# One transformer layer on one core: the cross-attention sums are turned by a transposing DMA and projected in fp16 pairs, and are normalised straight out of PSUM

## The reference, cut to what matters

```python
q = (x @ Wq).reshape(B, Nq, HEADS, DIM_HEAD).transpose(0, 2, 1, 3)
k = (context @ Wk)...                      # 16 heads of 64
v = (context @ Wv)...
sim = jnp.einsum('bhid,bhjd->bhij', q, k) * SCALE
attn = jax.nn.softmax(sim, axis=-1)
out = jnp.einsum('bhij,bhjd->bhid', attn, v)
out = out.transpose(0, 2, 1, 3).reshape(B, Nq, HEADS * DIM_HEAD)
return out @ Wo + bo
...
x = x + _L0_xattn_ref(_layernorm(x, axis=-1), ctx_768, ...)
```

## Time and profile before

| what | value |
|---|---|
| time, three runs | 2165.36, 2166.11, 2169.33 us, median 2166.11 |
| span of the profiled execution, which is its own time | 2169.9 us |
| mean granted TensorE clock | 0.997 |
| PE busy | 2103.3 us (97%) |
| POOL busy | 1933.6 us (89%) |
| ACT busy | 1832.2 us (84%) |
| DVE busy | 1736.7 us (80%) |
| transfers | 22.10 MB, mean 10 GB/s |

### The profile page before, as it was taken

One profiled execution on the slowest core, in us unless ns is written; L12 is line 12 of the kernel. 1 busy time (PEld: TensorE's weight loads), 2 busy tenths in 40 slices (PEclk: granted clock), 3 DMA queues, 4 the chain that ended last, 5 costly groups with the idle time before them and its releaser, 6 DMA issues.

```text
span 2169.9 us, 58374 instructions
## 1 busy us (share of the span) xinstructions
PE 2103.3 (97%) x22087; PEld 1544.3 (71%) x22087; DVE 1736.7 (80%) x4158; ACT 1832.2 (84%) x3124; POOL 1933.6 (89%) x1127
## 2 busy tenths in 40 slices
PE   8999999999999999999999999999999999999998
PEld 4677777777777777777777777777777777777665
DVE  7778878787887888879687797878878788886764
ACT  6898898989888888998888888898878888888872
POOL 3899999999999899999899998998989999899991
PEclk9999999999999999999999999999999999999999
DMA  3110000000000000000000000000000000000000
GB/s 73 42 38 13 2 13 2 2 13 2 13 2 2 13 2 13 2 13 2 11 13 2 13 2 2 14 2 13 2 11 13 2 13 2 2 2 2 2 11 11
DMA packets 17366, 22.10 MB, mean 10 GB/s; under 512 B 5872, under 2 KB 14976, under 8 KB 17088
## 3 DMA queue, kind: packets, MB, share of 16 engines
q1 hardware_dynamic: 15984, 18.17, 3.0%
q10 hardware_dynamic: 1104, 0.20, 0.1%
HBM read 16.14 MB, written 2.10 MB: 8 GB/s over the span
## 4 chain that ended last, share of the span: by engine, by line
PE 76%; DVE 11%; issue 5%; ACT 5%; POOL 2%; DMA 0%; SPq 0%; DVEq 0%; ACTq 0%; POOLq 0%
PE PS L573 14%; PE PS L613 13%; PE PS L574 13%; PE PS L590 11%; PE PS L592 10%; PE PS L636 4%; DVE EH L1091 4%; PE PS L646 2%; PE PS L623 2%; DVE over L1114 2%; POOL EL L1566 2%; ACT PF L897 2%; PE PS L657 1%; ACT over L919 1%; DVE junk L1359 1%
## 5 line engine op out<-in xcount | busy, mean ns | idle before, releaser
L1566 POOL TENSOR_TENSOR EL<-PF,EH 124x1024 f16<-124x1024 f32 x828 | 1761.7, 2153 | 144.0 <-DVE EH L1091 69.4
L897 ACT ACTIVATE PF<-PS 124x512 f32<-124x512 f32 x1664 | 972.6, 602 | 203.7 <-PE PS L574 190.1
L590 PE MATMUL PS<-Ch,EH 123*128 123x97 f16 (+1 forms) x6656 | 765.8, 207 | 22.9 <-POOL EL L1566 22.2
L592 PE MATMUL PS<-Cl,EL 123*128 123x97 f16 (+1 forms) x6656 | 762.3, 207 | 0.0
L1091 DVE TENSOR_SCALAR_CACHE_REDUCE EH<-PF 124x1024 f16<-124x1024 f32 x621 | 746.1, 1209 | 18.1 <-ACT PF L897 16.9
L590 PEld LDWEIGHTS PS<-Ch,EH 123*128 123x128 f16 (+1 forms) x6656 | 609.1, 98 | 181.5 <-issue 62.7
L1114 DVE CUSTOM_DVE_ANT_1 over<-over,PS 128x806 f32<-128x806 f32 x512 | 506.6, 989 | 284.7 <-ACT over L919 142.8
L592 PEld LDWEIGHTS PS<-Cl,EL 123*128 123x128 f16 (+1 forms) x6656 | 597.8, 98 | 168.2 <-issue 1.9
L573 PE MATMUL PS<-AH,ChT 97*124 97x512 f16 x1664 | 646.6, 389 | 6.5 <-ACT PF L897 5.8
L574 PE MATMUL PS<-AL,ClT 96*124 96x512 f16 x1664 | 633.7, 381 | 0.0
L919 ACT ACTIVATE over<-PS 128x806 f32<-128x806 f32 x512 | 433.4, 846 | 28.6 <-PE PS L613 8.6
(11 more groups left out here) (248 smaller groups left out, 1766.9 us busy)
## 6 DMA issues: line engine op xcount, KB each, us to landing
Cf<-in_ctx SPq DMA_DIRECT2D x16, 546.0 KB
X<-in_x SPq DMA_DIRECT2D x16, 128.0 KB, 2.4
out_x<-X SPq DMA_DIRECT2D x16, 128.0 KB, 1.7
msk<-in_attention_mask SPq DMA_DIRECT2D x4, 256.0 KB, 4.3
AH<-mh SPq DMA_DIRECT2D x63, 2.0 KB
Cf<-in_ctx SPq DMA_DIRECT2D x16, 53.6 KB
xWqT<-in_xWqT SPq DMA_DIRECT2D x2, 256.0 KB, 6.5
xWo<-in_xWo SPq DMA_DIRECT2D x2, 256.0 KB, 4.3
```

The source lines that it names most:

```text
L590: pe.matmul(PS[:, 6, u0:u0 + DC + 1], EH[0:kr, r, qs], Ch[j][0:kr, t, :], start=(t == 0 and q == 0), stop=False, skip_group_check=True)
L592: m = pe.matmul(PS[:, 6, u0:u0 + DC + 1], EL[0:kr, r, qs], Cl[j][0:kr, t, :], start=False, stop=(t == KT - 1), skip_group_check=True)
L897: act.activation(PF[:, n % PRING, :], PS[0:KP, 4 + n % 2, :], ACT.Exp).then_inc(sg("ex"), 1)
L1566: pool.tensor_tensor(EL[:, r - 1:r + 1, :], PF[:, f - 1:f + 1, :], EH[:, r - 1:r + 1, :], ALU.subtract).then_inc(sg("lo_pool"), 1)
```

## The change

- **Normalisation.** The copy `U` goes. VectorE reads the denominators and the sums from PSUM bank 6 itself, directly behind the last value product of a pair (place `n0`), and writes `Un` (fp32, one buffer for each of two pairs). TensorE waits on `un` instead of `u` before the next pair's first value product. The first three value products of a pair are now issued together at its third place, so two steps stand without one.
- **Split.** A new step `u_split` (place `n0+1`, GpSimd `n0+2`): ScalarE writes the high fp16 part of `Un`, GpSimd the low part, into `UHL`.
- **Turn.** `turn_u` is no step of TensorE, ScalarE or PSUM any more. It is one DMA on SP for each quad (place `n0+3`) with `transpose=True`: `UHL`, 128 partitions x 1536 fp16, into `UT`, 12 blocks of 128x128. SP gets an order of its own, with the stores of the output (`c_scat`) six places later.
- **Projection** (place `n0+11`): 12 fp16 products for each quad (high part with `MH`, low part with `ML`, for two row tiles and three blocks) instead of six fp32 ones; VectorE adds to `X` with a scale (`pback`).
- **Once, in the first batch** (places 34 to 39): the maximum of `M`, its power of two, the scaling of `M`, and the split into `MH` and `ML` (VectorE and ScalarE).
- **`sel_rank`.** The sum of two counts and the comparison that makes `keep` are written as `tensor_scalar` with an accumulator output.
- **Closing part.** The last quad goes the same way (`norm` on VectorE as before, then split, DMA, projection); the filler before the last `proj` is 24 products instead of 4 and 1.

The core of the diff:

```diff
+SPLIT_LATER, TURN_LATER, PROJ_LATER = 1, 3, 11
...
-            "ln_stats2": 3, "norm": 3},
+            "ln_stats2": 3, "u_split": 1},
+    "sp": {"c_scat": 6},
...
-        if late >= 1 and late % KT == 1:
+        if late >= 2 and late % KT == 2:
+            put(n, "av", late - 2)
             put(n, "av", late - 1)
-        if late >= 0 and late % KT:
+        if late >= 0 and late % KT >= 2:
             put(n, "av", late)
+        if late >= 0 and late % KT == KT - 1 and late // KT < B * HP - 1:
+            put(n, "norm", late // KT)
...
-        if done >= 2 and (done - 2) % KT == 0:
-            put(n, "norm", (done - 2) // KT)
-        for late, step in ((-2, ("turn_u", 0)), (2, ("turn_u", 1)), (5, ("proj",))):
...
+        if done >= 0 and done % KT == SPLIT_LATER:
+            put(n, "u_split", done // KT)
+        for later, kind in ((TURN_LATER, "turn_u"), (PROJ_LATER, "proj")):
+            if done >= 0 and done % (2 * KT) == KT + later:
+                quad = done // (2 * KT)
+                put(n, kind, quad // QD, quad % QD)
...
-                ("turn_u", B - 1, QD - 1, 0): 4, ("proj", B - 1, QD - 1): 1, ("sel_row", B - 1): 17,
+                ("proj", B - 1, QD - 1): 24, ("sel_row", B - 1): 17,
...
                     if t == 0 and n > 0:
-                        w.wait_ge(sg("u"), b * HP + hp)
+                        w.wait_ge(sg("un"), b * HP + hp)
...
+                    w.wait_ge(sg("ut"), 16 * i)
+                    kb = bank_free(s)
+                    w.wait_ge(sg("m_lo"), 1)
+                    for t in range(T):
                         for c in range(QC):
+                            for part, of in enumerate((MH, ML)):
+                                m = pe.matmul(PS[:, kb, t * D:(t + 1) * D], UT[:, (part * T + t) * QC + c, :],
+                                              of[:, qd * QC + c, :], start=(c == 0 and part == 0),
+                                              stop=(c == QC - 1 and part == 1))
...
+                elif k == "u_split":
+                    w.wait_ge(sg("un"), x + 1)
+                    w.wait_ge(sg("ut"), 16 * max(0, b * QD + qd - 1))
+                    act.activation(UHL[qd % 2][:, 0, :, 2 * (x % 2):2 * (x % 2) + 2, :], Un[x % 2][:, :, :, :],
+                                   ACT.Copy, scale=KEEP).then_inc(sg("uh"), 1)
...
+                elif k == "norm":
                     x, = s.a
                     sums = PS[:, 6, 0:4 * (DC + 1)].rearrange("p (q c) -> p q c", c=DC + 1)
+                    w.wait_ge(sg("av"), (x + 1) * KT)
+                    dve.reciprocal(rden_u[:, x % 2, :], sums[:, :, DC]).then_inc(sg("u_r"), 1)
+                    w.wait_ge(sg("u_r"), x + 1)
+                    if x >= 2:
+                        w.wait_ge(sg("ul"), x - 1)
                     dve.tensor_tensor(
+                        Un[x % 2][:, :, :, :].rearrange("p t h c -> p h t c"),
...
+                        ALU.mult).then_inc(sg("un"), 1)
...
-                    dve.tensor_tensor_reduce(out=rank[:, j, :], in0=cnt[:, j, 0, :], in1=cnt[:, j, 2, :], scale=1.0,
-                                             scalar=0.0, op0=ALU.add, op1=ALU.add, accum_out=spill())
-                    dve.tensor_scalar(keep[:, j, :], cnt[:, j, 1, :], NSEL + 0.5, None,
-                                      ALU.is_gt).then_inc(*own_step())
+                    for t in range(T):
+                        dve.tensor_scalar(rank[:, j, t:t + 1], cnt[:, j, 0, t:t + 1], cnt[:, j, 2, t:t + 1], None,
+                                          ALU.add, ALU.add, accum_out=spill())
+                    dve.tensor_scalar(keep[:, j, :], cnt[:, j, 1, :], NSEL + 0.5, None, ALU.is_gt, ALU.add,
+                                      accum_out=spill()).then_inc(*own_step())
...
+                    w.wait_ge(sg("uh"), x + 1)
+                    pool.tensor_tensor(UHL[qd % 2][:, 1, :, hs, :], Un[x % 2][:, :, :, :], UHL[qd % 2][:, 0, :, hs, :],
+                                       ALU.subtract).then_inc(sg("ul"), 1)
...
+                elif k == "turn_u":
+                    b, qd = s.a
+                    w.wait_ge(sg("ul"), b * HP + 2 * qd + 2)
+                    w.wait_ge(sg("pj_mm"), b * QD + qd)
+                    sp.dma_start(UT[:, :, :], UHL[qd % 2][:, :, :, :, :].rearrange("p w t h c -> p (w t h c)"),
+                                 transpose=True).then_inc(sg("ut"), 16)
```

More of the change, by code:

```diff
@@ L216, in put @@
         stream.append((n + shift.get(kind, 0), len(stream), (kind, *a)))
-    out += opening(engine)
+    out += opening("pe" if engine == "sp" else engine)
     groups, todo = beside_plan(), []
@@ L239, in whole_order @@
         done = n - AV_LAG - (KT - 1)
-        if done >= 2 and (done - 2) % KT == 0:
-            put(n, "norm", (done - 2) // KT)
-        for late, step in ((-2, ("turn_u", 0)), (2, ("turn_u", 1)), (5, ("proj",))):
-            late += KT
-            if done >= late and (done - late) % (2 * KT) == KT:
-                quad = (done - late) // (2 * KT)
-                put(n, step[0], quad // QD, quad % QD, *step[1:])
+        if done >= 0 and done % KT == SPLIT_LATER:
[4 more added lines that the diff above has]
+                put(n, kind, quad // QD, quad % QD)
     out += [step for _, _, step in sorted(stream)]
-    out += [("norm", B * HP - 1), ("turn_u", B - 1, QD - 1, 0), ("turn_u", B - 1, QD - 1, 1), ("proj", B - 1, QD - 1)]
+    out += [("norm", B * HP - 1), ("u_split", B * HP - 1), ("turn_u", B - 1, QD - 1), ("proj", B - 1, QD - 1)]
     out += [("ln_stats2", B - 1), ("sel_w", B - 1), ("sel_row", B - 1)]
@@ L261 @@
     "sa_t": "sa_xT", "sa_qk": "sa_k", "sa_v": "sa_vp", "sa_s": "sa_ex", "sa_turn": "sa_exT", "sa_o": "sa_x1",
-    "sa_f": "x2_lo", "wvo": "crow", "ctx_t": "ct", "q": "q_lo", "placemax": "pm_hi", "turn_u": "ut", "proj": "pj_x",
-    "sigma": "sg_max", "gtop": "gt_max",
+    "sa_f": "x2_lo", "wvo": "crow", "ctx_t": "ct", "q": "q_lo", "placemax": "pm_hi", "proj": "pj_x",
+    "sigma": "sg_max", "gtop": "gt_max", "mtop": "mt_max",
     "sel_row": "sel_cnt", "c_gather": "cg_mr", "c_turn": "c_mrT", "c_qkm": "c_rope", "c_val": "c_vx", "c_tqk": "c_kx",
@@ L395, in build @@
         qscale = sb("qscale", [P, 2, 4, 2])
-        U = [sb(f"U{i}", [P, 4, DC + 1]) for i in range(2)]
-        Un = [sb(f"Un{i}", [P, T, 4, DC]) for i in range(2)]
-        UT = sb("UT", [P, T, QC, P])
+        Un = [sb(f"Un{i}", [P, T, 2, DC]) for i in range(2)]
+        UHL = [sb(f"UHL{i}", [P, 2, T, 4, DC], F16) for i in range(2)]
+        UT = sb("UT", [P, 2 * T * QC, P], F16)
         pmax = sb("pmax", [P, 2, H * T])
@@ L552, in tensor_program @@
                 k, i = s.kind, s.i
-                if (k, *s.a) == ("turn_u", B - 1, QD - 1, 0):
+                if (k, *s.a) == ("proj", B - 1, QD - 1):
                     w.wait_ge(sg("ex"), TOTAL)
@@ L669, in tensor_program @@
                                  ident[0:KP, 0:KP]).then_inc(sg("sg_mm"), 1)
+                elif k == "mtop":
+                    w.wait_ge(sg("mmx"), 1)
+                    kb = bank_free(s)
+                    pe.transpose(PS[:, kb, 0:P], mmx[:, :].to_broadcast([P, P]), ident[:, :]).then_inc(sg("mt_mm"), 1)
                 elif k == "gtop":
@@ L1125, in vector_program @@
                                              op0=ALU.mult, op1=ALU.subtract).then_inc(sg("q_lo"), 1)
-                elif k == "norm" and s.a[0] == LAST_SUMS:
+                elif k == "norm":
                     x, = s.a
                     sums = PS[:, 6, 0:4 * (DC + 1)].rearrange("p (q c) -> p q c", c=DC + 1)
-                    w.wait_ge(sg("av"), TOTAL)
-                    w.wait_ge(sg("un"), x - 1)
-                    dve.reciprocal(rden_u[:, x % 2, :], sums[:, :, DC]).then_inc(*own_step())
-                    w.wait_ge(*own_steps())
-                    w.wait_ge(sg("ut_mm"), T * (B * QD - 2))
+                    w.wait_ge(sg("av"), (x + 1) * KT)
[3 more added lines that the diff above has]
+                        w.wait_ge(sg("ul"), x - 1)
@@ L1151, in vector_program @@
                 elif k == "proj":
                     b, qd = s.a
+                    back = pback[:, b % 2:b % 2 + 1]
+                    if qd == 0:
+                        w.wait_ge(sg("m_back"), 1)
+                        w.wait_ge(sg("sigma"), b + 1)
+                        if b >= 2:
+                            w.wait_ge(sg("pj_x"), at["proj", b - 2, QD - 1])
+                        dve.tensor_scalar(back, u_scale[:, b % 4:b % 4 + 1], mback[:, 0:1], None, ALU.mult, ALU.add,
+                                          accum_out=spill()).then_inc(sg("pj_back"), 1)
@@ L1647, in sync_program @@
             sp.dma_start(rbc[:, :], row("router_b")).then_inc(sg("in_rows"), 16)
-            for s in order:
+            for s in orders["sp"]:
                 k, i = s.kind, s.i
```

114 lines of the change are left out of this document (47 added, 67 removed).

## The result

The changed kernel takes 2243.89 us in the median (2241.81 to 2248.20), the kernel before beside it 2167.72. The ratio is 1.0353 with an interval of 1.0338 to 1.0368: some 77 us slower, where 48 us faster were forecast, and far outside the range of 2066 to 2172. The profiled execution spans 2242.8 us.

The account below looks back on a forecast made before the run. TensorE's issue order was taken as the bound, GpSimd 5% behind. TensorE's relief 66 plus 6 for `keep`, minus 24 of costs, gave 48 us: 2122 profiled, 2118 median, range 2066 to 2172.

Parts of the forecast that it names:

- the 2, 5 and 4 charged against it: Costs in the sum: 2 us for the opening batch, 5 for the closing part, 4 for stepping into the next bound.
- the sums' wait: TensorE's value products wait for the normalisation, or two bare score steps outrun ScalarE: 0.1 us a pair, 13 us.
- `keep`: VectorE's mask instruction loses its wait in accumulator form: 28 us of VectorE; a third of GpSimd's 17 us counted, 6.
- Relief of TensorE: TensorE's issue falls by 90 us, 5.6 a batch; 66 us come through: 8 short batches, 55 long, 3 first and last.
- GpSimd's 5%: GpSimd 95% busy in the short batch, so its work of 120.4 of 126.5 us leaves 6.1 us to gain.
- the length follows PE: From short to long batch TensorE's work grows 4.3 us, GpSimd's 2.4, length 5.7; TensorE's issue order is the bound.
- so no change: On GpSimd the normalising product (0.884 us) goes and the low-part subtraction, taken as 0.88, comes; ends -9 and +30 us.
- ACT's slack: ScalarE's 159.1 us of waiting for TensorE covers its share of the waits behind the split and normalisation.
- the sums' wait eats the gain: Rival: normalisation starts late on VectorE, TensorE stands at each pair's first value product; 2194 us; chance 0.19 with other stream waits.
- The DMA: Turning transfer of 384 KB for each quad lands in 5 us, costing nothing within 7.6 us of cover.
- The rival of the late DMA: Rival: the 12 blocks are turned one after another; landing at 14.4 us gives 2553 us; chance 0.07.
- Opening and closing part: One-time costs: 2 us for scaling and splitting in the opening batch, +4.7 us in the closing chain.

Follow-up runs that it names:

- n4: Changed kernel with GpSimd's low-part subtraction replaced by a one-element copy, the low part a constant zero: 2199.95 us, ratio 1.0134.
- n2: Changed kernel with GpSimd's low part two places later, nothing else: 2220.67 us, ratio 1.0231.
- n17: n4 with its one-element GpSimd copy two places later: ratio 1.0023 to the kernel before.
- n5: Changed kernel with the sums' old road, ranks and mask, low part a constant zero, DMA turn and fp16 projection kept but later: 2167.19 us, ratio 0.9989.
- n11: n5 with the new ranks and mask and a pair's first two value products together at the third step (two bare score steps): ratio 1.0035.
- n9: Kernel before with GpSimd's normalising product cut to a one-element copy, the normalised sums a constant: ratio 0.9963.
- n10: n5 with the new ranks and mask and GpSimd's normalising product cut to a one-element copy: ratio 0.9828.
- n6: Kernel before with only the value products of a pair's first two steps moved together to the third (two bare score steps): 2203.10 us, ratio 1.0158.
- n7: Kernel before with only the new ranks and keep mask (scalar operand and accumulator output): ratio 0.9988.
- n8: Changed kernel with the ranks and keep mask back in their old form: ratio 1.0366 to the kernel before.
- n12: n5 with the new ranks and mask and the normalising product on VectorE as four instructions of 96 columns: 2393.22 us, ratio 1.1033.
- n16: n5 with the new ranks and mask and every second pair's normalising product on ScalarE as four activations of 96 columns: ratio 1.0039.

## Why the prediction was wrong

Four kernels form a square: the low part's work there or not, its place early or late.

| | low part on GpSimd | one element |
|---|---|---|
| as changed | 1.0353 | 1.0134 (n4) |
| two places later on GpSimd | 1.0231 (n2) | 1.0023 (n17) |

The work costs 2.2 and 2.1%, its early place 1.2 and 1.1%, each whatever the other is. With them the loss adds up, in us: turn and fp16 projection -2 (n5); second bare step and the new ranks +10 (n11 to n5); straight normalisation and split against the old copy and GpSimd's product -3 (n17 to n11; the intervals overlap, and turn and projection also stand earlier in n17); the low part at a place where GpSimd stands for ScalarE's high part +24; the low part's work +48. Together +77.

The forecast was -48, so 125 us are missing. The first step below accounts for 53 of them: 66 less the 2, 5 and 4 charged against it make 55, and n5 measured 2. The second and third account for 69: I had nothing, and the runs have -3, +24 and +48. The rest, 3 us, is the sums' wait and `keep`.

- **Relief of TensorE, 66 us of 90 let through: this step failed.** The relief is there: twelve products take 0.67 us (466.22 to 466.89) for 0.69 forecast, and the transposes are gone. But n5 shows that it is worth 2 us beside the full GpSimd, and n9 and n10 that it is worth 29 beside a lighter one. Two readings of the earlier trace rows were wrong. GpSimd's 5% were no room of 6.1 us: its idle time is 6.1 us in the short batch and 9.4 in the long one before, and 5.8 and 9.2 in n5. That is mostly GpSimd standing for VectorE, which a lighter TensorE leaves as it is. And "the length follows PE" was a coincidence of sizes: from the short batch to the long one GpSimd's work grows by 2.4 us and its idle time by 3.3, which is the 5.7 us of length as well, and n5's long batch keeps its length with 4.3 us less of TensorE. For the eleven long batches I took 55 us; n5 has 14 there, and loses most of that again elsewhere. The 4 us for the step into the next bound were the term that should have held nearly all of it.
- **GpSimd, "so no change": this step failed too.** The subtraction took 0.92 us for the 0.88 taken, so in busy time the exchange was even. In time it was not: taking the product off gave 35 us beside n5 (n10), which the straight normalisation with ScalarE's split used up but for 3 (n17 to n11), and the subtraction's 118 us cost 48 (n4).
- **The waits behind `u_split`, for which "ACT's slack" was to cover: failed.** The queue that matters is not ScalarE's but GpSimd's, and its standing for ScalarE's high part is in no term of the sum. It stood 54.5 us in fourteen batches, and TensorE's value products waited 49.0 us for the late remainders, for 17.9. With the low part two places later 24 to 26 us came back (n17, n2).
- **The sums' wait, 13 us: the size right by luck, the mechanism half right.** The second bare step, which the prediction names, costs 10 us beside a lighter TensorE (n11) and 34 beside a full one (n6). The rival "the sums' wait eats the gain" did not come true as told: TensorE waited only 4.6 us for `Un` over the span. It had the sign, not the mechanism.
- **`keep`: the instruction as forecast, the gain not.** It takes 0.149 us now, but `X<-X,keep` behind it went from 348 to 1086 ns in the mean, and in n7 to 1179, so the 28 us of VectorE and the third of 17 us of GpSimd came to next to nothing (n7, n8). VectorE ended 79 us busier, not 45.
- **The DMA: right.** Landed after 3.7 us in the median (5.4 at most) for the 5 taken, far under the cover of 7.6; `proj` waited for one once, 1.40 us, in the closing part. The rival of the late DMA is out. The Trainium skill's figure of 1309 ns for a block (VectorE: DVE Perf Modes, section "The three transpose paths") added up block by block would have given 15.7 us; the runs show that blocks of one transfer don't add up so.
- **Opening and closing part: right.** The first batch took 137.6 us in n5 for 135.0, which is 2.6 where I had 2. In the closing part, from the end of the normalisation (2198.12) to the addition (2204.28) are 6.16 us for the 2.93 of before, +3.2 where I had +4.7.

What stays open: n17 has as light a GpSimd as n10 (1849.2 and 1856.1 us busy) and takes 42 us more. The second bare step is a part of it, somewhere between n11's 10 and n6's 34 us; the rest, up to 32 us, would be the straight normalisation with ScalarE's split, which no run takes apart. Whether a full version can beat the kernel before stays open as well: n10's 37 us need a place for the low part and the product that isn't GpSimd, and n12 and n16 found none.

## What to carry to other kernels

Where two engines pass tiles to each other in a chain and both are above nine tenths, relief of one alone may be worth little: here 2 and 8 us, against 37 for both. Price it by taking work off the second as well, before building the first. Idle time of the second engine is room only if it is spent waiting for the first; look at what ends each of its waits. On the engine with the least slack, an added instruction costs its own time and, if its input comes from another engine's queue, the time it stands at the head with the next stage's work behind it. Put it as late as its reader allows, which was one number and 26 us here. When a step is moved, look at what hangs on it: the normalisation one place later by itself cost 1.7%, and with the split behind it moved as well it cost nothing.

## What the runs showed of the hardware

A turning DMA of 384 KB (twelve blocks of 128x128 fp16) landed 3.7 us after its issue and held SP's queue for 1.45 us; as the tile's rows have it:

```profile
L1681 SPq DMA_TRANSPOSE UT<-UHL x64: 1414/1452/2562, 91.2 to 2199.7; - x64
...
DMA to landing us min/median/max: 3.6/3.7/5.4
```

A `tensor_scalar` of 96 columns with a scalar from SBUF and no accumulator output took from 253 to 2252 ns beside GpSimd's subtractions (n12), the 2.17 us of the earlier trace rows again. Where such a wait was removed by an accumulator output, it reappeared at the next instruction with two SBUF inputs (n7). The form isn't all: in the changed kernel `keep` in its old form took 157 ns at the median and `X<-X,keep` 967 in the mean (n8), so where the wait stands also goes by what runs beside it. The Trainium skill (SBUF — State Buffer, section "Who interferes with whom") has both kinds among those that contend with GpSimd, and the traces agree, with 2252 ns for the one (n12) and 2135 for the other (n7).
